# Stage one of a two-stage MetaFormer kernel: expert products with two experts stacked on the contraction and one image per column half

## The chip, the cores and the metric

The kernel runs on one core of a Trainium2 chip. The metric is the device time of one execution in microseconds (us); a value for the kernel is the median over its runs.

## What is computed

The input x has 8 images of 64 channels, 112 x 112 pixels, all in fp32. Two blocks follow each other:

```
x = x + window_attention(ln_c(x))           # 7x7 windows, one head, batch norm behind
t = tokens(x);  t = t + moe(ln_t(t))        # 8 experts of 64x64, top 2   <- stage one ends here
x = x + mamba_windows(ln_c(x))              # 8x8 windows, selective scan
t = t + expert_choice_ffn(ln_t(t))          # 32 experts, top 8 tokens of each
```

The part that the change touches is the first mixture of experts:

```
p = softmax(x_n @ router_w + router_b); top_p, top_i = top_k(p, 2); top_p /= sum(top_p)
expert_out[n, e] = x_n[n] @ expert_w[e] + expert_b[e]
out[n] = sum over the two chosen e of top_p[n, e] * expert_out[n, e]
```

The kernel computes it densely: every token goes through all eight experts, and the gate (zero for the six that weren't chosen) is multiplied onto x_n ahead of the product.

## The kernel before

Two images lie together on the 128 partitions (64 channels each; `x_v` pairs them). There are three stages with a barrier behind each: `phase_a` (attention and experts), `phase_b` (the scan), `phase_c` (the last experts). Setup, before them, loads and prepares the weights.

`phase_a` goes through 4 pairs of images by 16 strips of seven rows, 784 pixels (`TA`) each, 64 strips in all. Strips alternate between two slots (`SLOTS`); each engine runs `halves`, which calls its `half(s, it, m, im)`. One such half, called a **turn** here, does the attention of slot s and, interleaved with it, the experts of slot m, whose attention was done in the turn before. The order within a turn is written out by hand, separately for each engine, and engines meet through semaphores that count.

In a turn, TensorE (`half`, L582 on) does for slot s: centring strip (`strip`, L579), variance strip, product with the folded query and key weights (L607), scores of 16 windows (L624), values (L632), transposes (L640), window outputs (L654), again centring and variance (L579), and the router (L676). For slot m: gate transposes (L613), then for x = 0 to 7 a gate spread (`spread_gate`, L586) and an expert product (`experts`, L595), and last the expert biases (L671). `experts(lo, hi)` first waits for VectorE's product x, spreads the gate of x + 1, and only then multiplies by the weights of x.

The gate spread copies, for expert x, the gate of every token of image 0 to partitions 0 to 63 and that of image 1 to partitions 64 to 127 of the PSUM tile `pb` (weights `pick`: for x a 48x128 selection, three bf16 parts of the gate are summed). VectorE (L472) multiplies x_n by it and writes `a_xg`; two buffers per slot, so product x waits for expert x - 2. The weight of an expert (`w_exp`, 128x128) is block diagonal: the same 64x64 matrix for both images, zeros elsewhere. All eight products add up in the PSUM tile `pa`. In fp32 each matmul is recorded twice, since it goes through the array in two passes, and 784 columns take two banks (512 and 272 columns), so that an expert shows as x4.

VectorE's list in a turn: router chain of small operations for m, normalised strip into windows (L515), rest of the chain, product 0, row maximum (L532), product 1, subtraction (L537), product 2, sum and probabilities (L542 to L546), product 3, values plus shift (L552), products 4 and 5, x_1 (L558), products 6 and 7, x_n (L564), result of m (L568). ScalarE does squares (L414, L431), logarithms and exponentials of the variances (L416, L418, L433, L435), the exponential of the scores (L427) and copies out of PSUM (L420, L423, L429). GpSimd has nothing to do. The DMA queue of SP carries, for every strip, the load of x (`load`, L373, waits for x_1 of the strip before in that slot) and the store of the result (`store`, L377).

Stage two holds matmuls with fewer weight columns, on which the prediction draws: `strip` with `wx` (L1204, 128x64 weights), `out_proj` (L1261, 128x64 weights, image i into partitions 64i to 64i + 63) and `fold_row` (L1251, 128x32 weights into four quarters). Its SP queue also moves tiles within SBUF (`b_seq`).

Of the kernel before, what the change touches and what calls it, by code (L numbers as in the profile page):

```python
# [20 lines left out]
P = 128  # L21
# [32 lines left out]
def program(nc, x, wq, wk, wv, wo, gamma, beta, mean, var, router_w, router_b, expert_w, expert_b,  # L54
# [19 lines left out]
    with ExitStack() as top:  # L74
# [56 lines left out]
        w_router = sbuf("w_router", [P, 2 * NE], on=own)  # L131
        b_router = sbuf("b_router", [P, NE], on=own)
        rank8 = sbuf("rank8", [P, NE], on=own)
        w_exp = sbuf("w_exp", [P, NE, P], on=own)
        b_exp = sbuf("b_exp", [48, P], on=own)
        b_exp3 = sbuf("b_exp3", [48, 3, P], BF16, own)
        pick = sbuf("pick", [48, NE, P], BF16, own)
# [2 lines left out]
        with ExitStack() as st:  # L140
# [23 lines left out]
            for i in range(2):  # L164
                c0 = C * i
                loads += [
                    (wq2[:, i, :], wq), (wv2[:, i, :], wv),
                    (w_router[c0:c0 + C, NE * i:NE * i + NE], router_w),
                    (w_exp[c0:c0 + C, :, c0:c0 + C], expert_w.rearrange("e d c -> d e c")),
                    (pos_t[c0:c0 + C, :], pos.rearrange("a c h w -> (a c) (h w)")),  # L170
                    (w_in_t[c0:c0 + C, :], w_in),
                    (w_gate[c0:c0 + C, EC * i:EC * i + EC], gate_w.rearrange("e c -> c e")),
                    (b_gate[EC * i:EC * i + EC, :], gate_b.rearrange("(e a) -> e a", a=1)),
                ]
                for part in range(3):
                    r0 = 16 * part + NE * i
                    loads.append((b_exp[r0:r0 + NE, c0:c0 + C], expert_b))
# [16 lines left out]
            with nc.Block() as block:  # L194
                @block.sync
                def _(sp):
                    sp.wait_ge(zeroed, 8)
                    for dst, src in loads:
                        with nc.allow_non_contiguous_dma(reason="small weights, once"):
                            sp.dma_start(dst, src).then_inc(loaded, 16)  # L200
                    sp.wait_ge(loaded, 16 * len(loads))

                @block.gpsimd
                def _(pool):
                    g = nc.gpsimd
                    n = [0]

                    def link(ins):
                        n[0] += 1
                        ins.then_inc(masks, 1)  # L210
                        pool.wait_ge(masks, n[0])

                    def mark(t, pattern, base=0):

                        link(g.affine_select(out=t, in_=t, compare_op=ALU.not_equal, fill=1.0, base=base,
                                             pattern=pattern, channel_multiplier=1))

                    for t in (ident, ident_bf, pick, fold4, average, spread_b):
                        link(g.memset(t[:], 0.0))
                    link(g.memset(average[0:C, 0:C], 1.0 / C))  # L220
                    link(g.memset(average[C:P, C:P], 1.0 / C))
                    mark(ident[:], [[-1, P]])
                    mark(ident_bf[:], [[-1, P]])
                    mark(fold4[:], [[-1, 4], [-4, 32]])
                    for part in range(2):
                        mark(spread_b[:].rearrange("k m (j n) -> k m j n", n=4), [[-4, 4], [0, 32], [-1, 4]], -2 * NS * part)
                    for part in range(3):
                        mark(pick[:].rearrange("r e (i c) -> r e i c", i=2), [[-1, NE], [-NE, 2], [0, C]], -16 * part)
                    link(g.iota(rank8[:], pattern=[[-1, NE]], base=NE, channel_multiplier=0,
                                allow_small_or_imprecise_dtypes=True))  # L230

                @block.scalar
                def _(act):
                    act.wait_ge(zeroed, 11)
                    act.wait_ge(loaded, 16 * len(loads))

                    nc.scalar.activation(inv_row[:], bn_row[:, 3, :], ACT.Ln, bias=eps_bn[:]).then_inc(acts, 1)
# [13 lines left out]
                @block.vector  # L251
                def _(dve):
                    v = nc.vector
                    for t in (w_router, w_exp, b_exp, w_gate, w_qk, w_vo, w_z, w_conv):
                        v.memset(t[:], 0.0).then_inc(zeroed, 1)
                    v.memset(eps_bn[:], 1e-5).then_inc(zeroed, 1)
                    v.memset(eps_6[:], 1e-6).then_inc(zeroed, 1)
                    v.memset(one_col[:], 1.0).then_inc(zeroed, 1)
                    dve.wait_ge(zeroed, 11)
                    dve.wait_ge(masks, 17)  # L260
                    dve.wait_ge(acts, 3)
                    dve.wait_ge(prods, 3)
# [36 lines left out]
        def phase_a():  # L299
            HALF = SA // SLOTS  # L300
            with ExitStack() as st:
# [11 lines left out]
                sm = sb("a_sm", [P, NWA])  # L313
                x1 = sb("a_x1", [P, TA])
                xn = sb("a_xn", [P, TA])
                xg = [sbuf(f"a_xg{i}", [P, TA], F32, st) for i in range(2 * SLOTS)]
                res = sb("a_res", [P, TA])
                lg = sb("a_lg", [W, 2 * WIN, NE])
                ex = sb("a_ex", [W, 2 * WIN, NE])
# [21 lines left out]
                    sems(n) for n in ("xc2_", "sq2_", "var2_", "ln2_", "rstd2_", "xn"))  # L341
                rout_ready, expl_ready, gtr_ready, gt_ready = (sems(n) for n in ("rout", "expl", "gtr", "gt"))
                small = sems("small", SMALL)
                gate_ready, xg_ready, moe_ready = (sems(n, NE) for n in ("gate", "xg", "moe"))
                acc_ready, res_ready = sems("acc"), sems("res")
                nc.all_engine_barrier()

# [20 lines left out]
                with nc.Block() as block:  # L368
                    @block.sync
                    def _(sp):  # L370
# [4 lines left out]
                        def store(s, it):  # L375
                            sp.wait_ge(res_ready[s], it + 1)
                            sp.dma_start(x2[:, bass.ds(((it - 1) * SLOTS + s) * TA, TA)], res[s][:]).then_inc(stored[s], 16)  # L377

                        load(0, 0, 0, 1)
                        load(1, 0, 0, 1)  # L380
                        load(0, 0, 1, 2)
                        load(1, 0, 1, 2)
                        store(0, 1)
                        for k in range(NP):
                            with sp.Fori(0 if k else 2, HALF) as j:
                                it = j + (k * HALF + 1)
                                load(0, k, j, it)
                                store(1, it - 2)
                                load(1, k, j, it)
                                store(0, it - 1)  # L390
                        store(1, T - 1)
                        store(0, T)
                        store(1, T)
                        for s in range(SLOTS):
# [47 lines left out]
                    def _(dve):  # L442
# [5 lines left out]
                        def half(s, it, m, im):  # L448
# [17 lines left out]
                            def experts(lo, hi):  # L466

                                for x in range(lo, hi):
                                    dve.wait_ge(gate_ready[m], NE * im + x + 1)
                                    if x >= 2:  # L470
                                        dve.wait_ge(moe_ready[m], NE * im + x - 1)
                                    v.tensor_tensor(xg[2 * m + x % 2][:], xn[m][:], pb[m][:, 0:TA], ALU.mult).then_inc(xg_ready[m], 1)  # L472

                            if m is not None:

# [98 lines left out]
                    def _(pe):  # L574
# [7 lines left out]
                        def half(s, it, m, im):  # L582

                            def spread_gate(x):
                                for a, b in banks(TA):
                                    last = mm(pb[m][:, a:b], pick[:, x, :], gt[m][:, a:b], start=True, stop=True)  # L586
                                last.then_inc(gate_ready[m], 1)

                            def experts(lo, hi):
                                for x in range(lo, hi):  # L590
                                    pe.wait_ge(xg_ready[m], NE * im + x + 1)
                                    if x < NE - 1:
                                        spread_gate(x + 1)
                                    for a, b in banks(TA):
                                        last = mm(pa[m][:, a:b], w_exp[:, x, :], xg[2 * m + x % 2][:, a:b],  # L595
                                                  start=(x == 0), stop=False)
                                    last.then_inc(moe_ready[m], 1)

                            if s is not None:
# [961 lines left out]
```

## Time and profile before

| | |
|---|---|
| runs | 8925.04, 8931.17, 8936.10 us; median 8931.17 us |
| profiled execution | 8929.87 us, span 8928.1 us |
| TensorE (PE) busy | 6533.7 us, 73% of the span, 30290 matmul records |
| VectorE (DVE) | 6685.3 us, 75% |
| ScalarE (ACT) | 4407.7 us, 49% |
| GpSimd (POOL) | 5535.3 us, 62%, all but a little of it in stage two |
| granted TensorE clock, mean | 0.816 of 2.4 GHz |

Shares are averages over stages of different kind; a stage is read by its own windows. In a timeline a row is one instruction or several alike, with start, length, engine, line, tiles (out<-in), weights as rows*columns, shape and count; brackets hold the idle time before it and what ended it. A clock of 1.00 is 2.4 GHz, 0.50 is 1.2 GHz. Ends of matmuls are modelled, so starts are the surer times.

### The profile page before, as it was taken

The page shows a single profiled execution, that of the slowest core. Times are in us where ns is not written, and L with a number is a line of the kernel's source. Part 1 is how long each engine was busy: PE and PEld are TensorE (multiplying, and loading weights), DVE is VectorE, ACT ScalarE, POOL GpSimd, SP SyncE. Part 2 cuts the span into 40 slices and gives each one's busy share as a digit, 9 for nine tenths or more (in the row PEclk, how much of TensorE's full clock was granted, in tenths as well). Part 3 has the DMA queues.
Part 4 walks back from the last instruction along what each step waited for, and adds up shares of the span by engine and source line. Part 5 has one row for each costly group of instructions (what it writes and reads, how often), then busy time and mean ns, then how long its engine had stood idle before and what let it go on. Part 6 is the DMA issues. An engine that isn't in the chain of part 4 may idle for free. (4 is left out here: it accounts for less than half of the span.)

```text
span 8928.1 us, 102642 instructions
## 1 busy us (share of the span) xinstructions
PE 6533.7 (73%) x30290; PEld 2736.7 (31%) x30290; DVE 6685.3 (75%) x7811; ACT 4407.7 (49%) x5988; POOL 5535.3 (62%) x2731
## 2 busy tenths in 40 slices
PE   6888888888887666767676767776666766776555
PEld 3444444444443222222222222222222222222133
DVE  3555555555553999999999999999999999999633
ACT  1222222222222666666666667666666666666400
POOL 0000000000001999999999999999999999999700
PEclk8888888888887788887888888788888887788766
DMA  0000000000001555555555555555555555555553
GB/s 17 20 20 18 18 20 20 18 18 18 20 20 49 178 206 183 206 189 201 189 201 193 197 195 194 197 193 199 189 201 188 205 186 205 185 206 184 161 150 131
DMA packets 494003, 1202.18 MB, mean 135 GB/s; under 512 B 166501, under 2 KB 168713, under 8 KB 493705
## 3 DMA queue, kind: packets, MB, share of 16 engines
q1 hardware_dynamic: 493449, 1201.14, 39.2%
q0 software_dynamic: 512, 0.53, 0.0%
q8 instruction: 21, 0.34, 0.0%
q14 instruction: 21, 0.17, 0.0%
HBM read 943.43 MB, written 231.21 MB: 132 GB/s over the span
## 5 line engine op out<-in xcount | busy, mean ns | idle before, releaser
L1156 DVE TENSOR_TENSOR_SCAN b_h<-b_a,b_h 128x448 f32<-128x448 f32 x3584 | 3671.8, 1070 | 293.0 <-POOL b_h L981 145.2
L993 POOL TENSOR_TENSOR b_h<-b_h,b_ct 128x896 f32<-128x896 f32 x1792 | 3691.5, 2090 | 24.6 <-DVE b_h L1156 17.2
L1084 ACT ACTIVATE b_a<-b_dts,decay 128x441 f32<-128x441 f32 x3584 | 2226.6, 629 | 1583.6 <-DVE b_h L1156 1565.0
L1243 PE MATMUL b_b<-b_rows,spread_b 16*128 16x512 f32 (+1 forms) x1792 | 696.8, 785 | 1492.7 <-DVE b_h L1146 1491.7
L1004 POOL MEMSET b_seq<- 128x938 f32 x2 | 1.7, 882 | 2775.5 <-POOLq L768 2775.5
L1146 DVE TENSOR_TENSOR b_h<-b_dus,b_b 128x896 f32<-128x896 f32 x1344 | 1428.4, 1063 | 74.6 <-DMA b_dus<-d_dtu 71.5
L472 DVE TENSOR_TENSOR a_xg<-a_xn,a_pb 128x784 f32<-128x784 f32 x512 | 495.8, 968 | 632.7 <-PE a_pb L586 632.7
L1251 PE MATMUL b_y<-b_h,fold 128*32 128x512 f32 (+1 forms) x7168 | 956.8, 660 | 7.0 <-POOL b_h L993 7.0
L981 POOL TENSOR_TENSOR b_h<-b_dus,b_bt 128x896 f32<-128x896 f32 x448 | 936.1, 2090 | 10.7 <-DMA b_dus<-d_dtu 10.7
L595 PE MATMUL a_pa<-a_xg,w_exp 128*128 128x512 f32 (+1 forms) x2048 | 928.3, 581 | 0.0
L1243 PEld LDWEIGHTS b_b<-b_rows,spread_b 16*128 16x128 f32 x1792 | 167.0, 227 | 1761.4 <-DVE b_h L1146 1759.2
L1212 PE MATMUL b_w<-b_seq,w_conv 128*128 128x384 f32 (+1 forms) x896 | 540.7, 765 | 12.6 <-DMA b_seq<-b_seq 12.6
L595 PEld LDWEIGHTS a_pa<-a_xg,w_exp 128*128 128x128 f32 x2048 | 399.7, 215 | 489.5 <-issue 484.5
L1251 PEld LDWEIGHTS b_y<-b_h,fold 128*32 128x32 f32 x7168 | 217.1, 130 | 832.9 <-issue 679.8
L586 PE MATMUL a_pb<-a_gt,pick 48*128 48x512 bf16 (+1 forms) x1024 | 309.0, 389 | 78.7 <-ACT a_gt L423 77.7
L1212 PEld LDWEIGHTS b_w<-b_seq,w_conv 128*128 128x128 f32 x896 | 228.5, 268 | 377.7 <-issue 306.2
L431 ACT ACTIVATE a_sq<-a_pa 128x784 f32<-128x784 f32 x64 | 52.7, 824 | 507.1 <-PE a_pa L579 507.1
L429 ACT ACTIVATE a_pt<-a_pb 128x1024 f32<-128x1024 f32 x64 | 65.6, 1024 | 474.7 <-PE a_pb L640 474.7
L607 PE MATMUL a_pb<-a_xw,w_qk 128*128 128x512 f32 x256 | 150.5, 717 | 189.9 <-DVE a_xw L515 189.9
L1204 PE MATMUL b_w<-b_u,wx 128*64 128x512 f32 x448 | 276.5, 757 | 2.0 <-ACT b_dt L1027 2.0
L1212 PE MATMUL b_w<-b_seq,w_z 128*128 128x512 f32 x448 | 203.0, 575 | 91.8 <-ACT b_rows L1021 90.7
L427 ACT ACTIVATE a_p<-a_p 128x784 f32<-128x784 f32 x64 | 55.8, 871 | 425.6 <-DVE a_p L537 425.6
(209 smaller groups left out, 8870.8 us busy)
## 6 DMA issues: line engine op xcount, KB each, us to landing
b_bt<-d_rows SPq DMA_DIRECT2D x448, 448.0 KB, 6.0
b_ct<-d_rows SPq DMA_DIRECT2D x448, 448.0 KB, 3.7
b_dts<-d_dt SPq DMA_DIRECT2D x448, 448.0 KB, 6.0
b_dus<-d_dtu SPq DMA_DIRECT2D x448, 448.0 KB, 5.8
d_dt<-b_dt SPq DMA_DIRECT2D x112, 448.0 KB, 2.6
d_dtu<-b_soft SPq DMA_DIRECT2D x112, 448.0 KB, 2.5
b_seq<-b_seq SPq DMA_DIRECT2D x112, 234.0 KB, 3.4
a_x<-in_x SPq DMA_DIRECT2D x64, 392.0 KB, 3.1
```

The lines of the kernel that those rows point to most:

```text
L472: v.tensor_tensor(xg[2 * m + x % 2][:], xn[m][:], pb[m][:, 0:TA], ALU.mult).then_inc(xg_ready[m], 1)
L586: last = mm(pb[m][:, a:b], pick[:, x, :], gt[m][:, a:b], start=True, stop=True)
L595: last = mm(pa[m][:, a:b], w_exp[:, x, :], xg[2 * m + x % 2][:, a:b], start=(x == 0), stop=False)
L981: nc.gpsimd.tensor_tensor(hh[4 * m][:], dus[0][:], bt[m % 2][:], ALU.mult).then_inc(pb_done, 1)
L993: nc.gpsimd.tensor_tensor(hh[t][:], hh[t][:], ct[t // 4 % 2][:], ALU.mult).then_inc(hc_done, 1)
L1084: a(steps(bank(aa, k)), steps(half(dts[t % 4], k)), ACT.Exp, scale=decay[:, t % 4, t // 4:t // 4 + 1]).then_inc(a_done, 1)
L1146: v.tensor_tensor(hh[t][:], dus[t % 4][:], bb[:, 0:TB], ALU.mult).then_inc(b_done, 1)
L1156: v.tensor_tensor_scan(half(hh[t], k), bank(aa, k), half(hh[t], k), 0.0, ALU.mult, ALU.add).then_inc(h_done, 1)
L1204: last = mm(ww[rows, lo:hi], weight, src[:, lo:hi], start=True, stop=True)
L1212: last = mm(ww[:, lo:hi], weight, src[:, lo // ST:hi // ST, shift:shift + ST], start=(n == 0), stop=(n == len(weights) - 1))
L1243: last = mm(bb[:, lo:hi], spread_b[q, row, :], rows[i][q, lo:hi], start=True, stop=True)
L1251: last = mm(yy[32 * b:32 * b + 32, lo:hi], fold[:], hh[4 * row + b][:, lo:hi], start=False, stop=(row == 3))
```

## The change

Two experts are multiplied at once for one image. `w_exp` becomes 128 x 4 x 64: the upper 64 partitions hold the even expert of a pair, the lower 64 the odd one. The block diagonal and its zeroing go. For that, x_n of one image must stand on both halves of the partitions: a new tile `xd`, one per slot and image, is filled by four DMAs within SBUF per strip (`copies`, on SP's queue, behind a wait for x_n). `pick` is reordered so that step x spreads, for image x % 2, the gates of experts 2(x // 2) and 2(x // 2) + 1. VectorE still does eight products of 128x784 per strip, now from `xd`, into four `xg` buffers per slot, the first behind a wait for the four copies. TensorE's `experts` does a gate spread at every step, and at odd steps alone the product of the pair: for each bank two matmuls with 64 weight columns, image 0 into partitions 0 to 63 of `pa` and image 1 into 64 to 127.

```diff
-        w_exp = sbuf("w_exp", [P, NE, P], on=own)
+        w_exp = sbuf("w_exp", [P, NE // 2, C], on=own)
...
-                    (w_exp[c0:c0 + C, :, c0:c0 + C], expert_w.rearrange("e d c -> d e c")),
+                    (w_exp[c0:c0 + C, :, :], expert_w.rearrange("(p e) d c -> e d p c", e=2)[i]),
...
-                        mark(pick[:].rearrange("r e (i c) -> r e i c", i=2), [[-1, NE], [-NE, 2], [0, C]], -16 * part)
+                        mark(pick[:].rearrange("r n (e c) -> r n e c", e=2), [[-2, NE], [-1, 2], [0, C]], -16 * part)
...
-                    for t in (w_router, w_exp, b_exp, w_gate, w_qk, w_vo, w_z, w_conv):
+                    for t in (w_router, b_exp, w_gate, w_qk, w_vo, w_z, w_conv):
...
-                xg = [sbuf(f"a_xg{i}", [P, TA], F32, st) for i in range(2 * SLOTS)]
+                xd = [sbuf(f"a_xd{i}", [P, TA], F32, st) for i in range(2 * SLOTS)]
+                xg = [sbuf(f"a_xg{i}", [P, TA], F32, st) for i in range(4 * SLOTS)]
...
-                gate_ready, xg_ready, moe_ready = (sems(n, NE) for n in ("gate", "xg", "moe"))
+                gate_ready, xg_ready = (sems(n, NE) for n in ("gate", "xg"))
+                moe_ready, copied = sems("moe", NE // 2), sems("copied", 32)
...
+                        def copies(s, it):
+
+                            sp.wait_ge(xn_ready[s], it + 1)
+                            for i in range(2):
+                                src = xn[s][C * i:C * i + C, :]
+                                for e in range(2):
+                                    sp.dma_start(xd[2 * s + i][C * e:C * e + C, :], src).then_inc(copied[s], 16)
...
                                 it = j + (k * HALF + 1)
                                 load(0, k, j, it)
+                                copies(0, it - 1)
                                 store(1, it - 2)
                                 load(1, k, j, it)
+                                copies(1, it - 1)
                                 store(0, it - 1)
+                        copies(0, T)
                         store(1, T - 1)
+                        copies(1, T)
                         store(0, T)
                         store(1, T)
...
                                 for x in range(lo, hi):
+                                    if x == 0:
+                                        dve.wait_ge(copied[m], 64 * im + 32)
                                     dve.wait_ge(gate_ready[m], NE * im + x + 1)
-                                    if x >= 2:
-                                        dve.wait_ge(moe_ready[m], NE * im + x - 1)
-                                    v.tensor_tensor(xg[2 * m + x % 2][:], xn[m][:], pb[m][:, 0:TA], ALU.mult).then_inc(xg_ready[m], 1)
+                                    if x >= 4:
+                                        dve.wait_ge(moe_ready[m], NE // 2 * im + x // 2 - 1)
+                                    v.tensor_tensor(xg[4 * m + x % 4][:], xd[2 * m + x % 2][:], pb[m][:, 0:TA], ALU.mult).then_inc(xg_ready[m], 1)
...
-                                    last = mm(pb[m][:, a:b], pick[:, x, :], gt[m][:, a:b], start=True, stop=True)
+                                    last = mm(pb[m][:, a:b], pick[:, NE // 2 * (x % 2) + x // 2, :], gt[m][:, a:b], start=True, stop=True)
...
                                     pe.wait_ge(xg_ready[m], NE * im + x + 1)
                                     if x < NE - 1:
                                         spread_gate(x + 1)
+                                    if x % 2 == 0:
+                                        continue
                                     for a, b in banks(TA):
-                                        last = mm(pa[m][:, a:b], w_exp[:, x, :], xg[2 * m + x % 2][:, a:b],
-                                                  start=(x == 0), stop=False)
+                                        for i in range(2):
+                                            last = mm(pa[m][C * i:C * i + C, a:b], w_exp[:, x // 2, :], xg[4 * m + (x - 1) % 4 + i][:, a:b],
+                                                      start=(x == 1), stop=False)
                                     last.then_inc(moe_ready[m], 1)
```

TensorE, the start of a turn's expert work, from the wait for VectorE's product 0 to the one behind the value products (L591, L609 count registers); before:

```order
L586 MATMUL a_pb<-a_gt,pick 128x512 [waits a_xg0]
L586 MATMUL a_pb<-a_gt,pick 128x272
L595 MATMUL a_pa<-a_xg,w_exp 128x512
L595 MATMUL a_pa<-a_xg,w_exp 128x272
L591 REGISTER_ALU
L586 MATMUL a_pb<-a_gt,pick 128x512 [waits a_xg0]
L586 MATMUL a_pb<-a_gt,pick 128x272
L595 MATMUL a_pa<-a_xg,w_exp 128x512
L595 MATMUL a_pa<-a_xg,w_exp 128x272
L632 MATMUL a_pa<-w_vo,a_xw 128x128 [waits a_sub1]
L632 MATMUL a_pa<-w_vo,a_xw 128x128 x7
```

and now (L604 is the gate spread, L616 the expert product, L653 the value products):

```order
L604 MATMUL a_pb<-a_gt,pick 128x512 [waits a_xg0]
L604 MATMUL a_pb<-a_gt,pick 128x272
L609 REGISTER_ALU
L604 MATMUL a_pb<-a_gt,pick 128x512 [waits a_xg0]
L604 MATMUL a_pb<-a_gt,pick 128x272
L616 MATMUL a_pa<-a_xg,w_exp 64x512 x2
L616 MATMUL a_pa<-a_xg,w_exp 64x272 x2
L653 MATMUL a_pa<-w_vo,a_xw 128x128 [waits a_sub1]
L653 MATMUL a_pa<-w_vo,a_xw 128x128 x7
```

The product ahead of the second wait for `a_xg` is gone, and the one behind it has two matmuls per bank with 64 columns in place of one with 128.

SP's queue in the loop over strips, one slot, before (L373 load, L377 store):

```order
L373 ISA
L373 DMA a_x<-in_x 128x784
L376 REGISTER_ALU
L377 ISA
L377 DMA x<-a_res 128x784
L373 ISA
L373 DMA a_x<-in_x 128x784
L377 ISA
```

and now (L375 load, L387 copies, L379 store):

```order
L375 ISA
L375 DMA a_x<-in_x 128x784
L387 DMA a_xd<-a_xn 64x784 x4
L378 REGISTER_ALU
L379 ISA
L379 DMA x<-a_res 128x784
L375 ISA
L375 DMA a_x<-in_x 128x784
L387 DMA a_xd<-a_xn 64x784 x4
L379 ISA
```

Four copies have come between the load and the store of each slot.

## Rows read from the trace of the kernel before

**Rows 1.** One line, L595: count, ns min/median/max, first and last start in us.
```profile
L595 PE MATMUL a_pa<-a_xg,w_exp x2048: 392/592/1221, 118.8 to 2825.4; 128*128 128x272 f32 x94, 128*128 128x512 f32 x93
```

**Rows 2.** Windows, stage one: from:to, us, busy (x) of PE, PEld, DVE, ACT, POOL, clock, DMA share.
```profile
500.00:2500.00 2000.00, 1742.35 (x11593) 978.09 (x11592) 1036.51 (x1863) 423.72 (x513) 0.00 (x0) 0.87 0.06 19
```

**Rows 3.** Groups of the page: VectorE's gate products and what their idle time waited for.
```profile
L472 DVE TENSOR_TENSOR a_xg<-a_xn,a_pb 128x784 f32<-128x784 f32 x512 | 495.8, 968 | 632.7 <-PE a_pb L586 632.7
```

**Rows 4.** Timeline of TensorE over one turn: start us, us, engine, line, op.
```profile
1014.84 0.83 PE L586 MATMUL a_pb<-a_gt,pick 48*128 48x512 bf16 x2
1015.60 2.98 PE L595 MATMUL a_pa<-a_xg,w_exp 128*128 128x512 f32 x4
...
1019.27 2.50 PE L595 MATMUL a_pa<-a_xg,w_exp 128*128 128x512 f32 x4
1021.61 1.95 PE L632 MATMUL a_pa<-w_vo,a_xw 128*128 128x128 f32 x16
...
1023.92 1.58 PE L595 MATMUL a_pa<-a_xg,w_exp 128*128 128x512 f32 x4
...
1026.74 1.58 PE L595 MATMUL a_pa<-a_xg,w_exp 128*128 128x512 f32 x4
...
1028.69 1.58 PE L595 MATMUL a_pa<-a_xg,w_exp 128*128 128x512 f32 x4
1030.21 1.88 PE L654 MATMUL a_pb<-a_pt,a_vw 64*64 64x49 f32 x64
...
1033.88 1.48 PE L579 MATMUL a_pa<-a_x,center 128*128 128x512 f32 x4
...
1035.72 1.58 PE L595 MATMUL a_pa<-a_xg,w_exp 128*128 128x512 f32 x4
1037.14 1.48 PE L579 MATMUL a_pb<-a_sq,average 128*128 128x512 f32 x4
...
1041.52 1.55 PE L676 MATMUL a_pa<-w_router,a_xn 128*112 128x16 f32 x14 [0.49 <-DVE a_xn L564]
```

**Rows 5.** Windows of TensorE, same turn: from:to, us, PE busy (x), granted clock, DMA, GB/s.
```profile
1014.80:1021.20 6.40, 6.40 (x13) 0.50 0.00 0
1021.20:1042.00 20.80, 20.31 (x144) 1.00 0.06 19
```

**Rows 6.** Timeline of TensorE: first and last of 64 router blocks.
```profile
96.45 2.80 PE L676 MATMUL a_pa<-w_router,a_xn 128*112 128x16 f32 x14 [2.90 <-DVE a_xn L564]
...
2797.00 1.55 PE L676 MATMUL a_pa<-w_router,a_xn 128*112 128x16 f32 x14 [0.49 <-DVE a_xn L564]
```

**Rows 7.** Timeline of TensorE in stage two: strips and fold with fewer weight columns.
```profile
4095.36 3.25 PE L1204 MATMUL b_w<-b_u,wx 128*64 128x512 f32 x4
4098.54 2.39 PE L1251 MATMUL b_y<-b_h,fold 128*32 128x512 f32 x16
...
4997.89 3.25 PE L1261 MATMUL b_w<-b_yz,w_out_t 128*64 128x512 f32 x8
```

**Rows 8.** Windows of TensorE in stage two, columns as in rows 5.
```profile
4095.30:4098.50 3.20, 3.20 (x5) 0.50 0.00 0
4997.90:5001.10 3.20, 3.20 (x13) 0.50 0.71 224
```

**Rows 9.** Timeline of VectorE, same turn as rows 4.
```profile
1014.95 0.97 DVE L532 TENSOR_REDUCE a_mx<-a_pa 128x16 f32<-128x784 f32 x1 [2.62 <-PE a_pa L624]
1015.84 0.96 DVE L472 TENSOR_TENSOR a_xg<-a_xn,a_pb 128x784 f32<-128x784 f32 x1
...
1040.49 0.97 DVE L564 TENSOR_TENSOR a_xn<-a_pa,a_sq 128x784 f32<-128x784 f32 x1 [3.69 <-ACT a_sq L435]
```

**Rows 10.** Timeline of ScalarE, same turn.
```profile
1035.39 0.82 ACT L431 ACTIVATE a_sq<-a_pa 128x784 f32<-128x784 f32 x1 [7.95 <-PE a_pa L579]
```

**Rows 11.** DMA issues of stage one and of stage two: KB each, us to landing.
```profile
a_x<-in_x SPq DMA_DIRECT2D x47, 392.0 KB, 3.1
...
b_seq<-b_seq SPq DMA_DIRECT2D x20, 234.0 KB, 3.3
```

More of the change, by code:

```diff
@@ L196, in _ @@
                 def _(sp):
-                    sp.wait_ge(zeroed, 8)
+                    sp.wait_ge(zeroed, 7)
                     for dst, src in loads:
@@ L233, in _ @@
                 def _(act):
-                    act.wait_ge(zeroed, 11)
+                    act.wait_ge(zeroed, 10)
                     act.wait_ge(loaded, 16 * len(loads))
@@ L258, in _ @@
                     v.memset(one_col[:], 1.0).then_inc(zeroed, 1)
-                    dve.wait_ge(zeroed, 11)
+                    dve.wait_ge(zeroed, 10)
                     dve.wait_ge(masks, 17)
@@ L381, in _ @@
                         load(0, 0, 1, 2)
+                        copies(0, 1)
                         load(1, 0, 1, 2)
+                        copies(1, 1)
                         store(0, 1)
```

## The prediction

> **What bounds the kernel now.** I read the expert line and a window of the stage first: stage one (the window attention and the eight experts) shows its first expert product at 118.8 us and its last at 2825.4 us, and from 500 to 2500 us TensorE is busy 1742 of 2000 us at a granted clock of 0.87 on average, VectorE 1037 [rows 1, 2]. Next I looked at who waits: VectorE's gate products idle 632.7 us behind TensorE's gate spreads [rows 3], so the engine ahead of them is the late one. Then I laid out one turn of the stage on TensorE [rows 4]. From 1014.84 us to the router block at 1041.52 us (0.49 us idle ahead of it) no row shows a wait. Each of the rows of L595 is one expert. An expert costs 2.91 us of TensorE's time at the low clock (1015.60 to 1018.51, the next row's start) and 1.42 to 1.52 us at the high one. The windows give the clock: 0.50 (1.2 GHz) up to 1021.2 us, 1.00 (2.4 GHz) behind it [rows 5]. A turn (one `half` of the code) lasts from one router block to the next: 96.45 to 2797.00 us with 63 turns between, 42.87 us each [rows 6]. The whole stage is a chain of 63 such turns, closed by barriers, so what one turn gains the end gains, 63 times.
>
> **What a pair of experts costs in the new form.** Before, one expert is a 128x128 block-diagonal weight over 784 columns, in two banks, each matmul recorded twice because fp32 passes twice. After, a pair of experts has, for each bank, two matmuls with 64 weight columns, one for each image, writing partitions 0 to 63 and 64 to 127. Their number is the same as before; the gain exists only if the two run at the same time. The trace holds the same form in stage two. One strip of 128x64 weights over 896 columns, 4 records, takes 3.18 us to the next row at clock 0.50 (4095.36 to 4098.54). The output projection, also 128x64 and 896 columns, but for two images in the two column halves, 8 records, shows 3.25 us at the same clock 0.50 [rows 7, 8]. Twice the records in the same time: the halves overlap. The fold, four quarters of 32 columns with 16 records, shows 2.39 us [rows 7], no more than a single strip, and agrees. So I price a pair like one expert of today: 2.91 us cold, 1.42 to 1.52 us warm.
>
> The pair sits between gate spreads of the full width, so TensorE changes its tiling twice for each pair. In the rows a change costs nothing: the gate spread at 1014.84 lasts 0.83 us and the expert, with the same 128 columns, starts 0.07 us before that ends (ends are modelled) [rows 4]; the strip of 64 columns at 4095.36 lasts 3.25 us and the fold, another tiling, starts likewise 0.07 us before its end [rows 7]. I add nothing. The Trainium skill, page "TensorEngine Tiling (Array Packing)", section "Tiling Modes", says that changing the tiling mode drains TensorE. The Trainium skill, page "TensorE: Matmul & The Clock Gate", section "Step-by-step: what each phase is for", puts a drain at about 128 cycles; by those, as an estimate, eight changes in a turn would take 0.4 us, 27 us in all, and the time would be near 8684. The trace does not show that price, so the sum stays.
>
> **The turn written again, from 1014.84 us.** I keep the clock as it was (low until 1021.2) and walk through TensorE's list.
> - Of the eight expert blocks, four go (those of the even steps, at 1015.60, 1023.92, 1028.69 and 1035.72): 2.91 + 1.42 + 1.52 + 1.42 = 7.27 us.
> - The first one had covered a wait. The second gate spread now ends at 15.67, but the next one needs VectorE's product, which stands behind the row maximum (1014.95, 0.97 us) and ends itself at 1016.81 [rows 9]. TensorE waits from 15.60 to about 16.87: 1.27 us back.
> - The first pair then runs 17.63 to 20.54, wholly at the low clock, where expert one of today is half warm (1019.27 to 1021.61, 2.34 us): 0.57 back. The value products (1021.61, 1.95 us) begin at 20.54 and have 0.66 us of low clock: 0.33 back.
> - The fourth and fifth products of VectorE come 0.15 and 0.10 us late for their next gate spreads: 0.25 back.
> - The statistics strip at 1037.14 waits for ScalarE's square, 0.82 us behind the centring strip [rows 10]. The expert between them had covered that; now only a gate spread (0.83 us at the low clock, about half of it at the high one) does: 0.55 back.
> - The window products (L654), the second centring strip and the last pair follow without a wait; the statistics strip starts 4.3 us earlier, and from there (logarithm, exponential, x_n, router) nothing changes.
> Sum: 7.27 - 1.27 - 0.57 - 0.33 - 0.25 - 0.55 = 4.30 us per turn. Times 63: 271 us. The last gate phase stands alone; there VectorE's loop becomes the limit for every other expert, about 2 us more gained.
>
> **What is added.** VectorE does the same eight products of the same size, only from x_d. The new wait on the copies stands at the head of the first product; behind it are the row maximum and everything else on VectorE. The copies start when x_n is ready (1041.46: start 1040.49 plus 0.97 [rows 9]), one turn ahead: for the products near 1013.9 that is 998.6. So they have 15 us. Four copies of 196 KB are no row of the trace. By the nearest: two loads of 392 KB at 3.1 us are 6.2 us; by the move within SBUF in stage two (234 KB, 3.3 us) it is 784/234 times that, 11.1 us [rows 11]. Both lie inside 15 us, so they cost nothing; the first is the likelier, since stage two's moves share the engines with much other traffic. If the cover were gone, each microsecond over 15 costs one per turn. On the DMA queue (SP) they stand between a load that waits for x_1 and a store that waits for the result; x_n comes between these two, so the store moves back by the issue of four, and its buffer is not wanted for two turns. Setup: one zeroing fewer and smaller weight loads, under 1 us, counted as nothing.
>
> The profiled execution took 8929.87 us, 1.3 under the median of the runs shown (8931.17). 8929.87 - 271 - 2 = **8657 us**.
>
> **Rivals.**
> - *The clock comes back earlier or falls less* (0.16). Both column halves stream at once, so the pair keeps the array at least as busy as one expert does. If the low stretch ended 2.5 us earlier, some 1.3 us more is gained: 5.6 us per turn, 8575.
> - *The clock comes back later* (0.12). The new wait of 1.27 us lies in the cold stretch. If the clock came back 3.5 us later, half of that is lost, 1.7 us: 2.6 per turn, 8766.
> - *The clock stays low through the turn* (0.05), the one on the slower side. Its place is 1021.2 to 1042.0, where TensorE is busy 20.31 us at the high clock [rows 5]. With some 4.4 us of experts gone 15.9 stay; at the low clock the wide ones double (an expert 1.42 to 2.91) and the small ones grow less, so about 14 us come on top of a gain of 4.3. If it held in all turns: 63 x 9.7, 9541. It decides from three turns in ten; at half of them the time would be some 9100. For it speaks that the new TensorE is less busy; against it, that two column halves at once are no less work per microsecond than one full array, and that after 1021.2 the new list has only waits of 0.10 to 0.55 us.
> - *The halves do not overlap, so the change does not do what it says* (0.02). Then 7.27 comes back and the waits shrink to about 1.5 us per turn: 9024. The overlap shown above speaks against it [rows 7, 8].
> - *The copies land late* (0.03). At 20 us they cost 5 us per turn: 8970, slower; at 16 us, 8720.
> - The forecast itself: 0.62.
>
> **How the numbers follow.** The forecast, its two neighbours on the clock (8575 and 8766) and part of the copies' case give the range 8560 to 8780; left out are the clock staying low, the serial halves, late copies beyond some 2 us and the ends beyond the neighbours. 0.2% of this kernel is 18 us, about what a measurement tells from no change. Faster: 0.62 + 0.16 + 0.12 + 0.02 of the copies' 0.03 + a little of the clock case, 0.93. Same: 0.01. Slower: 0.06.
>
> **What would show it.** In the new profile: eight records of 128x64 in 2.9 us cold and 1.5 us warm for a pair; busy time of the expert group at somewhat over half of today's; router blocks 38.6 us apart; VectorE's wait for copies absent or under 0.1 us; a wait of about 1.3 us before the third gate spread, ended by VectorE. The prediction is wrong if pairs take 2.9 us warm, if the clock in the stage falls well below 0.87, or if the first gate product waits on a DMA.

## The result, and the profile after

The changed kernel takes 8796.4 us (median of 4 runs, 8781.2 to 8807.6) against 8928.1 us: 0.9846 of the time before, 95% interval 0.9834 to 0.9858. That is 132 us less where 273 had been forecast (4.30 us in each of 63 turns and 2 us at the end), and above the range of 8560 to 8780 us. The profiled execution took 8805.53 us, span 8803.7 us.

Stage one in the windows, and VectorE's gate products, after; they answer to [rows 2] and [rows 3]:

```profile
500.00:2500.00 2000.00, 1657.25 (x12069) 868.66 (x12070) 1079.29 (x1952) 443.88 (x536) 0.00 (x0) 0.79 0.14 39
```

```profile
L490 DVE TENSOR_TENSOR a_xg<-a_xd,a_pb 128x784 f32<-128x784 f32 x512 | 495.3, 967 | 637.7 <-PE a_pb L604 635.5
```

TensorE is busy 1657 us of 2000 instead of 1742, and its granted clock fell from 0.87 to 0.79. No gate product waits for a transfer: all of its listed idle time ends with TensorE's gate spread (L604).

One turn on TensorE, in the form of [rows 4]; L616 is a pair of experts, L604 a gate spread:

```profile
1029.03 1.55 PE L697 MATMUL a_pa<-w_router,a_xn 128*112 128x16 f32 x14 [0.34 <-DVE a_xn L582]
...
1032.91 1.58 PE L597 MATMUL a_pb<-a_sq,average 128*128 128x512 f32 x4 [0.91 <-ACT a_sq L430]
1037.46 3.78 PE L628 MATMUL a_pb<-a_xw,w_qk 128*128 128x512 f32 x4 [2.97 <-DVE a_xw L533]
1041.17 0.85 PE L634 MATMUL a_pb<-ident_bf,a_g 112*48 112x112 bf16 x7
1043.06 0.83 PE L604 MATMUL a_pb<-a_gt,pick 48*128 48x512 bf16 x2 [1.04 <-ACT a_gt L439]
1043.82 3.65 PE L645 MATMUL a_pa<-a_xw,a_t 64*64 64x49 f32 x64
1047.41 0.83 PE L604 MATMUL a_pb<-a_gt,pick 48*128 48x512 bf16 x2
1049.43 0.83 PE L604 MATMUL a_pb<-a_gt,pick 48*128 48x512 bf16 x2 [1.19 <-DVE a_xg L490]
1050.19 2.88 PE L616 MATMUL a_pa<-a_xg,w_exp 128*64 128x512 f32 x8
1053.00 2.35 PE L653 MATMUL a_pa<-w_vo,a_xw 128*128 128x128 f32 x16
...
1057.28 1.54 PE L616 MATMUL a_pa<-a_xg,w_exp 128*64 128x512 f32 x8
...
1061.54 1.54 PE L616 MATMUL a_pa<-a_xg,w_exp 128*64 128x512 f32 x8
1063.01 1.58 PE L597 MATMUL a_pa<-a_x,center 128*128 128x512 f32 x4
1064.53 0.50 PE L604 MATMUL a_pb<-a_gt,pick 48*128 48x512 bf16 x2
1065.51 1.58 PE L597 MATMUL a_pb<-a_sq,average 128*128 128x512 f32 x4 [0.48 <-ACT a_sq L447]
1067.02 1.54 PE L616 MATMUL a_pa<-a_xg,w_exp 128*64 128x512 f32 x8
...
1069.99 1.55 PE L697 MATMUL a_pa<-w_router,a_xn 128*112 128x16 f32 x14 [0.34 <-DVE a_xn L582]
```

The pairs cost what was forecast: 2.81 us at the low clock (1050.19 to 1053.00) and about 1.5 us at the high one, for eight records. The wait ahead of the third gate spread is there too: 1.19 us in brackets at 1049.43, ended by VectorE's product. The first and last router block of the 64 give the turn:

```profile
96.51 1.56 PE L697 MATMUL a_pa<-w_router,a_xn 128*112 128x16 f32 x14 [2.90 <-DVE a_xn L582]
...
2667.43 1.55 PE L697 MATMUL a_pa<-w_router,a_xn 128*112 128x16 f32 x14 [0.34 <-DVE a_xn L582]
```

(2667.43 - 96.51) / 63 = 40.81 us, where 42.87 was the turn before [rows 6] and 38.57 the forecast. So a turn gained 2.06 us on average and not 4.30; 63 x 2.06 = 130 us. The clock within the turn, to compare with [rows 5]:

```profile
1030.40:1036.70 6.30, 3.18 (x10) 0.99 0.69 181
1036.70:1053.70 17.00, 14.01 (x92) 0.50 0.00 0
1053.70:1071.40 17.70, 16.80 (x150) 1.00 0.09 27
```

The low stretch lasts 17 us here, from the wait for the window strip (2.97 us idle ahead of 1037.46) through the first pair into the value products. It looks so in each turn between 500 and 2500 us: 42% of that time is at 1.2 GHz (called the **low share** from here on), against 25% before. Router blocks there are 40.95 to 40.97 us apart every time, where they had been 41.5 to 46.8.

The same kernel has other turns, though. In this profile three of them, between the router blocks at 261.28 and 373.72 us, last 37.48 us each. The windows below are whole turns, from router block to router block: first two neighbouring ones of the kernel before, then one of these three and one of the later ones (from:to, us, PE busy (x), granted clock, DMA share, GB/s).

```profile
956.24:997.74 41.50, 35.77 (x247) 0.92 0.06 19
997.74:1041.52 43.78, 38.37 (x247) 0.84 0.05 18
```

```profile
298.76:336.24 37.48, 30.15 (x248) 0.91 0.16 43
1029.03:1069.99 40.96, 33.95 (x247) 0.79 0.15 39
```

The two turns of the changed kernel hold the same work. What differs is the clock: by its mean it was low for about 7 us of the first and 17 us of the second. The turn of 41.50 us in the kernel before also has about 7 us at the low clock. At equal low time the change is therefore worth 41.50 - 37.48 = 4.02 us a turn, close to the 4.30 forecast.

### The profile page after: what moved, and what is told of

The parts are those of the page before. It is cut to its first block and busy times, and to the rows that moved or that the text cites. A ratio compares the mean times of both kernels' runs of the same rounds, so it can differ in the third digit from the quotient of the medians.

```text
span 8803.7 us, 102835 instructions
## 1 busy us (share of the span) xinstructions
PE 6314.4 (72%) x30290; PEld 2534.8 (29%) x30290; DVE 6682.1 (76%) x7810; ACT 4408.5 (50%) x5988; POOL 5536.3 (63%) x2731
## 5 line engine op out<-in xcount | busy, mean ns | idle before, releaser
L490 DVE TENSOR_TENSOR a_xg<-a_xd,a_pb 128x784 f32<-128x784 f32 x512 | 495.3, 967 | 637.7 <-PE a_pb L604 635.5
L616 PE MATMUL a_pa<-a_xg,w_exp 128*64 128x512 f32 (+1 forms) x2048 | 477.5, 595 | 1.1 <-DVE a_xg L490 1.1
L604 PE MATMUL a_pb<-a_gt,pick 48*128 48x512 bf16 (+1 forms) x1024 | 317.4, 398 | 153.0 <-DVE a_xg L490 80.0
L628 PE MATMUL a_pb<-a_xw,w_qk 128*128 128x512 f32 x256 | 233.8, 1066 | 190.0 <-DVE a_xw L533 190.0
L597 PE MATMUL a_pb<-a_sq,average 128*128 128x512 f32 (+1 forms) x512 | 208.3, 530 | 89.6 <-ACT a_sq L430 58.5
```

What stands on the lines that cost most here:

```text
L490: v.tensor_tensor(xg[4 * m + x % 4][:], xd[2 * m + x % 2][:], pb[m][:, 0:TA], ALU.mult).then_inc(xg_ready[m], 1)
L604: last = mm(pb[m][:, a:b], pick[:, NE // 2 * (x % 2) + x // 2, :], gt[m][:, a:b], start=True, stop=True)
L616: last = mm(pa[m][C * i:C * i + C, a:b], w_exp[:, x // 2, :], xg[4 * m + (x - 1) % 4 + i][:, a:b], start=(x == 1), stop=False)
```

## The experiments

Two theories to begin with. **A**: the pairs bring what they should, and the longer low stretch takes half of it back. **B**: the copies, the tiling changes or the new waits take it. Each ratio is against runs of the kernel before on the same chip. Where a turn's length or a low share is given without a row, it is the mean over the turns between 500 and 2500 us of the trace, a turn being the distance from router block to router block; blocks likewise, from their start to the next one's. The `+` lines of fillers stand behind tests (both slots at work) that are left out here, and `...` marks lines left out.

### e1 and e2: the idle time at the turn's start filled, in both kernels

```diff
+ def filler(dst, sizes):
+     for n in sizes:
+         mm(dst[:, 0:n], center[:], w_conv[:].rearrange("p a b c -> p (a b c)")[:, 0:n], start=True, stop=True)
  strip(pa[s], center[:], xt[s]).then_inc(xc_ready[s], 1)
+ filler(pb[m], (384,))
  pe.wait_ge(sq_ready[s], it + 1)
  strip(pb[s], average[:], sq[s]).then_inc(var_ready[s], 1)
+ filler(pb[m], (512, 512, 512))
...
  last.then_inc(gtr_ready[m], 1)
+ filler(pa[s], (384,))
```

> The changed kernel, with additional fp32 matmuls on constants into free PSUM tiles where TensorE waits at a turn's start: 384 columns behind the first centring strip, 3 x 512 behind the variance strip, 384 behind the gate transposes. They only occupy TensorE. Theory A (the shortfall of 2.5 us per turn is the clock, low for 42% of the stage instead of 26%): the granted clock in 500 to 2500 us rises from 0.79 to over 0.95, the query and key product falls from 3.71 to about 1.9 us, the scores from 3.58 to 2.6, the first pair from 2.81 to 1.5, and a turn lasts 35.5 to 36.5 us: 8796 - 63 x 5 = about 8480 us, range 8440 to 8540. Theory B (the shortfall comes from the copies, the tiling changes or the new waits): the clock is not what limits, and the fillers bring under 0.5 us per turn or cost time: 8770 to 8850.

> The same fillers in the kernel before. Theory A: it too loses the low stretch (query and key 2.26 to 1.9 us, scores 3.14 to 2.6, first expert 2.91 to 1.45, second 1.97 to 1.42, gate spreads 0.76 to 0.43): a turn of about 39 us, 8928 - 63 x 3.7 = about 8695 us. The gap to the changed kernel with fillers is then what the change is worth at one clock, 3.5 to 4.3 us per turn, 220 to 270 us; the 132 us measured are that less the longer low stretch. Theory B: the gap stays at 132 us.

Measured: e1 8601.5 us, 0.9625 (0.9609 to 0.9641); e2 8689.6 us, 0.9725 (0.9709 to 0.9741). Work that computes nothing made both kernels faster, so the clock limits both; for e2 the forecast held to 5 us. For e1 it didn't. Its turn is 37.55 us, and the trace shows why:

```profile
1013.73 0.50 PE L608 MATMUL a_pb<-a_gt,pick 48*128 48x512 bf16 x2
1015.75 0.50 PE L608 MATMUL a_pb<-a_gt,pick 48*128 48x512 bf16 x2 [1.52 <-DVE a_xg L490]
1016.19 2.76 PE L620 MATMUL a_pa<-a_xg,w_exp 128*64 128x512 f32 x8
1018.87 2.47 PE L663 MATMUL a_pa<-w_vo,a_xw 128*128 128x128 f32 x16
```

The gate spreads before the pair run at the high clock (0.50 us), then TensorE waits 1.52 us for VectorE, and the pair behind it takes 2.76 us, the time of the low clock. This suggests that the new wait brings the clock down by itself, even where the turn's start is filled (the low share is 0.14). e7 below tests it.

### e3 and e4: the copies taken away, and added alone

```diff
# e3, from the changed kernel (no call of copies, no wait for them)
- v.tensor_tensor(xg[4 * m + x % 4][:], xd[2 * m + x % 2][:], pb[m][:, 0:TA], ALU.mult)
+ v.tensor_tensor(xg[4 * m + x % 4][:], xn[m][:], pb[m][:, 0:TA], ALU.mult)
# e4, from the kernel before: copies(s, it) as in the change, and
+ if x == 0:
+     dve.wait_ge(copied[m], 64 * im + 32)
```

> The changed kernel without the four copies and the wait for them; VectorE multiplies x_n itself (both images) in all eight products. Left out: the doubled x_n, so the pair's gates meet the wrong operand. Theory A: no transfer was ever waited for, so the turn stays at 40.96 us and the time at 8796 us, within 20. Theory B (the copies disturb SBUF accesses or the loads): 20 to 120 us less than 8796.

> The kernel before with the four copies per strip and VectorE's wait for them, their result unused. Theory A: 8928 us within 20, no wait of VectorE on a transfer, low clock share as before (26%). Theory B: it is 50 to 120 us slower than 8928, which would be the share of the copies in the shortfall.

Measured: e3 8791.2 us, 0.9840 (0.9823 to 0.9856), with a turn of 40.96 us and every block between 500 and 2500 us as long as in the changed kernel to within 0.01 us (ahead of 500 us its profile has ten of the turns of 37.5 us, where that of the changed kernel has three); e4 8931.3 us, 0.9998 (0.9988 to 1.0007). The copies cost nothing in either direction; that part of B falls.

### e5: the order of the change without its saving

```diff
# from the kernel before; product buffers: 4 per slot
+ if x % 2 == 0:
+     continue
+ for y in (x - 1, x):
      for a, b in banks(TA):
-         last = mm(pa[m][:, a:b], w_exp[:, x, :], xg[2 * m + x % 2][:, a:b], start=(x == 0), stop=False)
+         last = mm(pa[m][:, a:b], w_exp[:, y, :], xg[4 * m + y % 4][:, a:b], start=(y == 0), stop=False)
```

> The kernel before, with TensorE's order and the four product buffers of the changed one: even steps spread a gate only, odd steps multiply two experts, but each expert with its own 128x128 weights as before; no copies. All the work of the kernel before, plus the new wait ahead of the third gate spread. Theory A1 (the new wait in the low stretch, and not the halved expert work, keeps the clock low longer): low share of 500 to 2500 us rises from 0.26 to 0.35 or more, a turn of 45 to 46.5 us, 9070 to 9170 us. Theory A2 (the lower load of TensorE does it): the low share stays near 0.26 and only the wait itself is paid, some 1.3 us per turn: about 9010 to 9040 us.

Measured: 8973.4 us, 1.0044 (1.0028 to 1.0061); the low share is 0.25, the turn 43.41 us. The order alone costs 40 us, less than either theory said, and doesn't lengthen the low stretch. A1 (the new wait alone keeps the clock low) falls. In this trace the wait is there (1.18 us) and the clock comes back all the same, in the two experts that follow it (4.50 us; two at the low clock would be 5.8):

```profile
1029.23 0.83 PE L586 MATMUL a_pb<-a_gt,pick 48*128 48x512 bf16 x2 [1.18 <-DVE a_xg L472]
1029.99 4.50 PE L598 MATMUL a_pa<-a_xg,w_exp 128*128 128x512 f32 x8
1034.33 1.95 PE L635 MATMUL a_pa<-w_vo,a_xw 128*128 128x128 f32 x16
```

### e6 and e9: work in the new wait alone

```diff
# from the changed kernel, in TensorE's experts
+ if x == 1 and s is not None:
+     filler(pb[s], (512,))        # e9: (384,)
  pe.wait_ge(xg_ready[m], NE * im + x + 1)
```

> The changed kernel with one filler only, 512 columns in the new wait ahead of the third gate spread (1.7 us at the low clock, so 0.5 us longer than the wait). Theory A1: the clock returns one step earlier, turn 39.5 us or less, 8700 us or less. Theory A2: the low stretch begins at the start of the turn and stays as long as it is; the turn is 41 to 41.5 us, 8800 to 8830 us.

> The changed kernel with a filler of 384 columns (1.28 us at the low clock) in the new wait, about as long as the wait of 1.26 us, so that it adds work but next to no time. Theory C1 (it is the work in the wait that brings the clock back): as with 512 columns, a turn of 38.0 to 39.0 us, 8630 to 8690 us. Theory C2 (it was the 0.5 us of delay that moved the turn against the clock's steps and broke an unlucky alignment, in which every turn was 40.96 us to within 0.01): the turn stays at 40.96 us, 8796 us.

Measured: e6 8665.4 us, 0.9701 (0.9685 to 0.9718), turn 38.49 us; e9 8630.8 us, 0.9666 (0.9650 to 0.9682), turn 38.22 us. The low share is 0.23 and 0.22. One matmul of filler per turn (two records, in fp32) brings the turn to the forecast's 38.57 us or under it. It acts at two places. Behind it the value products are at the high clock (2.05 us in e9, below). And at the start of the following turns the clock stays high longer: the query and key product takes 2.07 us (e6) and 2.13 us (e9) on average, where it takes 3.71 us in the changed kernel.

```profile
1031.96 0.83 PE L608 MATMUL a_pb<-a_gt,pick 48*128 48x512 bf16 x2
1032.72 1.65 PE L597 MATMUL a_pb<-w_conv,center 128*128 128x384 f32 x2
1034.30 0.83 PE L608 MATMUL a_pb<-a_gt,pick 48*128 48x512 bf16 x2
1035.06 2.28 PE L622 MATMUL a_pa<-a_xg,w_exp 128*64 128x512 f32 x8
1037.27 2.05 PE L659 MATMUL a_pa<-w_vo,a_xw 128*128 128x128 f32 x16
```

This is A1 in its number (39.5 us or less). e5 has the wait without the halved experts, at a low share of 0.25, and e11 below the halved experts without the wait, at 0.27. The changed kernel has both and 0.42. So neither alone gives the long low stretch; both together allow it, though they don't force it, as the three turns of 37.48 us show.

### e10: the same place, time without work

```diff
# from the changed kernel, VectorE's products
+ if x == 1:
+     v.tensor_copy(spare[m][:, 0:384], one_col[:].broadcast_to([P, 384]))
```

> The changed kernel with a VectorE copy of 384 columns into a spare tile (about 0.46 us) ahead of product 1, which makes the new wait longer by as much and gives TensorE no work. C1: no gain, 8796 to 8850 us (0 to 0.5 us per turn added, low share 0.40 or more). C2: as with the 512-column filler, a turn of 38.5 to 39.5 us, 8660 to 8720 us, low share under 0.30.

Measured: 8801.9 us, 0.9865 (0.9849 to 0.9881), low share 0.36, turn 40.51 us. The delay did break up the even turns (they are 37.7 to 44.1 us long now), and it brought nothing. The filler of e9 took 1.58 us and not the 1.28 expected, so it too is a delay, and about as long a one as e10's: from the second gate spread to the third it is 2.34 us in e9 (1031.96 to 1034.30) and 2.29 us in e10 (1055.87 to 1058.16), where it had been 2.02 us. So for a delay of this size it is the work in the wait that counts (C1), and not its timing (C2); other delays weren't tried.

### e7, e8 and e11: all waits filled; the new wait removed by order

```diff
# e8 and e11, TensorE: gate 1 between the two halves of the scores
  for w in range(NWA):
+     if w == NWA // 2 and m is not None:
+         pe.wait_ge(xg_ready[m], NE * im + 1)
+         spread_gate(1)
...
- experts(0, 2)
+ if s is None:
+     experts(0, 1)
+ experts(1, 2)
# e8 and e11, VectorE: product 1 ahead of the row maximum
- experts(0, 1)
+ experts(0, 2)
...
- experts(1, 2)
```

e7 is e1 with the filler of e6; e8 has this order and e1's fillers, e11 this order and no filler.

> The fillers of the first run and this one together. The first run left short low stretches at the pair behind the new wait (first pair 2.43 us on average, value products 2.61, where 1.5 and 1.9 are the high-clock times) and at the first strips (2.01 for 1.40). If it is the clock that the new wait brings down there, these go: turn 35.3 to 36.3 us, 8600 - 63 x 1.8 = about 8490 us, and the gap to the kernel before with fillers grows from 88 to about 200 us, 3.2 us per turn. If not, 8590 to 8610 us.

> The changed kernel with the three fillers of the first run, and the new wait taken away by order instead of filled: TensorE spreads gate 1 in the middle of the scores, VectorE does product 1 ahead of the row maximum. Then gate spread 2 and the first pair run while VectorE takes the maximum and subtracts. Turn 34.5 to 35.5 us at the high clock, 8600 - 63 x 2.5 = about 8440 us, range 8400 to 8500. If the clock at that place doesn't hang on the wait, only the wait of 1.5 us is gained: 8505.

> The changed kernel with the reordering of the last run (gate 1 within the scores, product 1 ahead of the row maximum) and no filler at all, so no work that isn't the reference's. The wait of 1.26 us is gone. If the clock behaves as in the turn of the kernel before (low from the wait for the window strip to the middle of the first pair), a turn of 37.3 to 38.3 us, 8570 to 8630 us. If the turn stays in the alignment of the changed kernel, it gains the wait alone or nothing: 8720 to 8796 us.

Measured: e7 8496.1 us, 0.9513 (0.9497 to 0.9529), turn 35.88 us; e8 8451.2 us, 0.9459 (0.9443 to 0.9475), turn 35.07 us; e11 8645.7 us, 0.9689 (0.9672 to 0.9705), turn 38.27 us. e7 and e8 came within 11 us of their forecasts. e7 shows that it was the new wait in e1: with it filled, the first pair takes 1.47 us in every turn, where e1 has 2.43 on average. In e8 the gate spread ahead of the pair has no wait and the pair its high-clock time (a wait of 0.72 us for VectorE has opened ahead of the transposes instead):

```profile
1025.83 0.50 PE L606 MATMUL a_pb<-a_gt,pick 48*128 48x512 bf16 x2
1026.26 1.14 PE L656 MATMUL a_pa<-a_xw,a_t 64*64 64x49 f32 x32
1027.40 0.50 PE L606 MATMUL a_pb<-a_gt,pick 48*128 48x512 bf16 x2
1027.83 1.54 PE L618 MATMUL a_pa<-a_xg,w_exp 128*64 128x512 f32 x8
1029.48 2.05 PE L666 MATMUL a_pa<-w_vo,a_xw 128*128 128x128 f32 x16
```

e11 is the best without work that the reference doesn't need, 0.9689 of the kernel before where the changed kernel is 0.9846, about 140 us better; it lies 16 us above its range. Its low share is still 0.27; with the waits at the turn's start filled as well (e8) it is 0.08. Of all versions e8 is the fastest.

The windows of TensorE from 500 to 2500 us (columns as above) show work and clock of e2, e7, e9 and e10, in this order:

```profile
500.00:2500.00 2000.00, 1920.12 (x13239) 0.98 0.06 20
```

```profile
500.00:2500.00 2000.00, 1799.93 (x13629) 0.96 0.18 49
```

```profile
500.00:2500.00 2000.00, 1683.29 (x13068) 0.89 0.16 42
```

```profile
500.00:2500.00 2000.00, 1628.79 (x12155) 0.82 0.15 40
```

## Why the prediction was wrong

**The step that failed** is "I keep the clock as it was (low until 1021.2)". It was taken from one turn, the one of 43.78 us above, and held fixed while the work around it was changed. What the runs showed in its place: between 500 and 2500 us the clock goes low earlier, stays low for 17 us of each turn, and costs about 2.3 us of the 4.30. Block by block, means over 46 turns before and 47 after, in us from a block's start to the next:

| block | before | after | forecast of the difference | measured |
|---|---|---|---|---|
| four expert blocks removed | 7.27 | 0 | -7.27 | -7.27 |
| wait ahead of the third gate spread | 0 | 1.26 | +1.27 | +1.26 |
| first pair for the second expert | 1.97 | 2.81 | +0.57 | +0.84 |
| value products | 1.88 | 2.28 | +0.33 | +0.40 |
| wait for ScalarE's square (in the gate spread's block) | 0.43 | 0.98 | +0.55 | +0.55 |
| late products of VectorE (transposes, second pair) | 2.49 | 2.72 | +0.25 | +0.23 |
| query and key product | 2.26 | 3.71 | 0 | +1.45 |
| gate spread 0 and scores | 3.72 | 4.35 | 0 | +0.63 |
| the rest | | | 0 | +0.11 |
| turn | 42.75 | 40.96 | -4.30 | -1.80 |

The two blocks at the turn's start, to which the working gave nothing, hold 2.08 of the missing 2.50 us. They are ahead of 1014.84, where it began: they ran partly at the high clock before, and between 500 and 2500 us never do after. (From the first to the last router block the gain is 2.06 and not 1.80 a turn. The stage before opens with a turn of 47.8 us, and the changed one has its three turns of 37.48 us. The forecast's 4.30 was put against the turn of 42.87 us.) In those three turns, with the same order, waits and sizes, the query and key product takes 1.91 us and the scores 2.3 to 2.4 us, and the turn is 1.1 us shorter than forecast. So the sum lacks no large term but the clock.

**What held.** That a pair costs as much as one expert, taken from stage two's output projection [rows 7, 8]: 2.81 us low and 1.47 us high, against 2.91 and 1.42 to 1.52 [rows 4]. The wait of 1.27 us, the two late products, the wait for the square. That the copies have room: they are issued from 1029.01 us on, within 2.42 us, one lands 3.4 us behind its issue (median), and the first gate product that reads them starts at 1044.00, 15.0 us later. e3 and e4 show that they cost nothing.

```profile
a_xd<-a_xn SPq DMA_DIRECT2D x192, 196.0 KB, 3.4
```

**The tiling changes.** The working gave them nothing; the estimate that it set aside was 27 us. With the clock high in both kernels (e7 against e2) the blocks that border on a pair are longer: the pair itself 1.47 for 1.42, the value products 1.98 for 1.88, the second centring strip 1.52 for 1.41, the strip of statistics behind it 1.51 for 1.32. Summed over a turn (0.05 four times, 0.10, 0.11, 0.19), less 0.15 at the expert biases, that is 0.45 us, 28 us in 63 turns. Not all of this is the tiling. e5 has the changed order with full-width experts; its value products take 1.88 us and its second centring strip 1.41, but its strip of statistics, which stands behind the same wait, takes 1.42:

```profile
1048.85 1.58 PE L579 MATMUL a_pb<-a_sq,average 128*128 128x512 f32 x4 [0.48 <-ACT a_sq L431]
1050.27 2.80 PE L598 MATMUL a_pa<-a_xg,w_exp 128*128 128x512 f32 x8
```

So 0.10 of the 0.19 came with that wait, and 0.35 us a turn, 22 us in all, is what comes with the narrow pairs. The Trainium skill, page "TensorEngine Tiling (Array Packing)", section "Tiling Modes", says that changing the tiling mode drains TensorE. The prediction's estimate from that rule was 27 us, so the longer blocks fit it in size; that they are the drain was not tried by itself. The reading of the rows by which a change cost nothing was wrong. The row at 1014.84 changes no column tiling, and at 4098.54 the fold stands behind a semaphore (in the trace its weight load waits 1.18 us for GpSimd). The 0.07 us by which a block starts before the modelled end of the last shows at longer blocks too (1061.54 and 1.54 us, next start 1063.01), so it tells nothing of a price.

**At one clock.** Between e2 and e7, with the clock at 0.98 and 0.96, the change is worth 0.9725 - 0.9513 = 0.0212 of 8934 us, 189 us or 3.0 us a turn (38.92 against 35.88). That is the forecast's own sum with all experts at the high clock: 5.95 us removed, less a wait of 1.59, 0.55 for the square, some 0.2 for late products and the 0.45 of longer blocks, 3.2; these last terms are read from the same two traces. It is less than at equal low time (4.02), since the removed experts are cheaper at the high clock. So the mechanism was right; the term that was mis-sized is the clock, about 2.3 us of the missing 2.5 per turn (2.08 at the turn's start, up to 0.34 in the first pair and the value products, part of which is the tiling).

**The rivals.** "The clock comes back later" had the mechanism and 8766 us as its time, at a chance of 0.12; the clock in fact also went low earlier in the turn. (By its own 2.6 us a turn it would be 8764; the 2 us of the last phase were left out.) It should have had more: the trace of before showed turns of 41.5 to 46.8 us, so the low stretch was known not to be a constant. "The clock comes back earlier" (5.6 us a turn) is what the three turns of 37.48 us did (5.4), before the kernel left them for good.

**What stays open.** Which amount of work in the wait suffices, and why the changed kernel leaves the turns of 37.48 us for those of 40.96 and stays there, with the low clock always beginning at the same place, no run here settles. e10 shows that breaking the even turns up by one delay gains nothing. The four times of the changed kernel lie 26 us apart, as would seven or eight turns of the shorter kind more or less; that this is their cause is not shown, since one profile was kept.

## What to carry to other kernels

Where TensorE's clock is low for part of a loop, write the turn down at both clocks before costing an edit, and ask which waits the removed work had covered: a wait that opens in the low stretch can cost more than its length. When work leaves TensorE, close the wait that it opens, by order if another engine's list allows (e11, about 140 us), and look whether idle time at the start of a turn can hold work. And a price for switching between shapes is to be read from start to start, where matmuls follow without a wait, beside the same block with equal neighbours.

## What the runs showed of the hardware

Matmuls on constants in idle time made the kernel before 2.75% faster (e2) and the changed one 3.4% faster than it was (e7 against the changed kernel: 0.9513 to 0.9846). With 0.91 and 2.97 us of idle time at the turn's start (busy 3.18 of 6.30 us in the window above) the clock fell ahead of the query and key product in every turn of the changed kernel between 500 and 2500 us. The same idle time didn't always do so: in the turns at 298.76 (changed) and 956.24 (before) that product still took 1.91 us, at 2.4 GHz, and the clock fell only during the scores. With fillers there the low share is 0.14 (e1) and 0.04 (e2). One kernel can run its turns at 37.48 and at 40.96 us, by the clock alone. A single wait of 1.52 us between full-speed blocks, behind the scores, was followed by a pair at 1.2 GHz (e1); with work in it the pair stayed at 2.4 GHz (1.47 us, e7). Two column halves of 64 run at once in stage one as in stage two: 8 records in the time of 4.
